# A four-block cross-attention transformer step: the first FFN's first two pairs of tiles moved into the last attention slot and its tail

## The chip, the cores and the metric

The kernel runs on one core of a Trainium2 chip. A core has four compute engines, each with its own instruction queue: TensorE (PE, matrix products, writes to PSUM only), VectorE (DVE), ScalarE (ACT) and GpSimd (POOL); SyncE (SP) issues DMAs. They run side by side and wait for each other through semaphores. The metric is the device time of one execution in microseconds, the median of several runs.

## The reference

The input x is 4 batches of 512 tokens of 128 features. Four blocks follow, each with a cross-attention (16 heads of 8, 77 keys) and an FFN, each of a different kind:

```
x = x + tanh(g) * attention_l(layernorm(x), ctx)      # l = 0..3
x = x + tanh(g) * ffn_l(layernorm(x))
```

What matters here is the end of the first attention and the first FFN. Its three products have both operands rounded to a 4-bit grid in blocks of 16 values:

```
def fp4_quant_dequant(x):        # blocks of 16 along the last dim
    scale = max(|xb|) / 6;  q = nearest of {0,.5,1,1.5,2,3,4,6} * sign * scale
gate = q(x) @ q(w_gate).T;   y = q(x) @ q(w_up).T
h    = silu(gate) * y                                 # 352 wide
out  = q(h) @ q(w_down).T
```

So for each token the input is rounded, two products are made, silu and a product follow, the result is rounded again and multiplied down to 128 features.

## The kernel before

The 2048 tokens are 16 tiles of 128; a batch b has four tiles (TPB = 4). The attention of block l runs in slots k = -1 to 4, and each slot has NCH = 12 steps c. In slot k TensorE makes the turned scores of batch k (turned_scores), ScalarE their exponentials (weigh, L783), TensorE the weighted sums (L1665, in three groups, the last one in step 0 of the next slot), and, one slot later, the tail of batch k: turn_sums (transposes of the sums), VectorE's normalise, att_transposed, ScalarE's attT_out, project, and VectorE's residual_read and residual with the statistics of the next layer norm. Slot k = B = 4 holds only the tail of batch 3. GpSimd refines the inverse deviation (refine, L582 to L585) and makes the shift (shift), and ScalarE normalises with them (normalise_out, L724).

The FFN of block 0 (ffn0 on each engine) goes by pairs of tiles, j = 0 to 7. For a pair:

- TensorE: up(2j), up(2j+1) (L1747, L1748: gate and up products into banks 0 to 3). An fp32 product shows as two records of the trace.
- ScalarE: silu of both tiles (L850).
- VectorE: product(j) (L1326), its blockwise maximum (L1330), rounded(j): the 4-bit rounding in eight operations (L981 to L983, L973 to L977).
- GpSimd: one multiplication with the scales (L677).
- TensorE and ScalarE: turn(i) (L1755, transposes in bank 4), hT_out(i) (L854, L855), down(i) (L1764), for the tiles of a pair two turns of the loop later. There is one bank for the turned tiles, so turn(i) waits for hT_out(i - 1).

product(j) for j >= 2 waits for the turns up to tile 2j - 3, and up(2j) waits for product(j - 1). Behind rounded(3) and rounded(5) stand residual(0) and residual(1) on VectorE; in turns j = 5 and 7 TensorE also makes the input and the queries of block 1 (turn_input, queries).

The FFN's input, batch by batch, has its own rounding. Batches 0 to 2 are jobs 3 to 5, shared between VectorE (job_scales, L994 and L981 to L983; job_steps, L1001 and L1002) and GpSimd (quantise_begun, quantise_ended, L609 to L616), in slots 2, 3 and 4. Batch 3 is done by VectorE alone in ten operations, quantise_batch(3) (L1098 to L1101), behind product(1). Then input_transposed(b) (TensorE, L1737) and xqT_out(b) (ScalarE, L844) turn a batch; they stand in turns j = 0, 1, 3 and 5 of the FFN's loop.

Every engine carries out its instructions in the order in which the program issues them, and that order is written by hand: functions such as after(k, c) on VectorE say what comes in which step. An instruction that waits holds all that is behind it on its engine.

Of the kernel before, what the change touches and what calls it, by code (L numbers as in the profile page):

```python
# [94 lines left out]
def program(nc, a, out):  # L95
    with ExitStack() as ctx:
# [223 lines left out]
        def tail_bank(n, h): return 7 if n == N - 1 and h == 1 else 3  # L320
# [178 lines left out]
        def _(pool):  # L499
# [117 lines left out]

            pool.wait_ge(ld_const, 16)
# [12 lines left out]
            for l in range(L):  # L631
                for k in range(-2, B + 1):
                    n = l * B + k
                    if l == 0 and k == 1:
                        quantise_begun(2)
                        quantise_ended(2)
                    if 0 <= k < B and n + 2 < N and n + 2 >= 3 * B:
                        mask_rows(n + 2)
                    if 0 <= k < B and n + 3 < N:
                        key_rows(n + 3)  # L640
                    if 0 <= k + 1 < B:
                        split_maxima(n + 1)
                    if l == 0 and k == 0:
                        for j in range(2):
                            quantise_begun(j)
                            quantise_ended(j)
                    if l == 0 and k >= 2:
                        quantise_begun(k + 1)
                        quantise_ended(k + 1)
                    if l == 2 and k == -1:  # L650
                        refine((5, B - 1))
                        shift((5, B - 1))
                    if l == 2 and k == -1:
                        pool.wait_ge(am_w_part, 1)
                        pool.partition_all_reduce(am[:, 3:4], am[:, 1:2], P, RMAX).then_inc(am_w_all, 1)
                    if l == 0 and k in (-1, 1, 3):
                        mask_parts((k + 1) // 2)
                    if l == 1 and k in (-1, 0, 2):
                        mask_parts((3, 4, 0, 5)[k + 1])
                    if l == 1 and k == 1:  # L660
                        last_masks()
                    if l == 2 and k == 0:
                        split_experts(gH, gL, 0)
                    if l == 2 and k == 1:
                        split_experts(uH, uL, 1)
                    if k >= 1:
                        refine((2 * l + (l > 1) + 1, k - 1))
                        if l == 0:
                            shift((1, k - 1))
                    if l == 3 and 1 <= k <= 3:  # L670
                        split_down(k - 1)
                if l == 0:
                    for j in range(T // 2):
                        h = fh[:, j % 2, :, :].rearrange("p t (n e) -> p (t n) e", e=16)
                        v = qh[:, j % 2, 0, :].rearrange("p (n e) -> p n e", e=16)
                        pool.wait_ge(hq_scaled, j + 1)
                        pool.tensor_tensor(h, v, hscale[:, j % 2, :].unsqueeze(2).to_broadcast([P, 44, 16]),  # L677
                                           ALU.mult).then_inc(hq_done, 1)
# [18 lines left out]
        def _(act):  # L697
# [54 lines left out]
            def attention(l):  # L752
# [50 lines left out]
                for k in range(-1, last + 1):  # L803
                    for c in range(NCH):
# [35 lines left out]

            def ffn0(xT_one, q_one):
                def xqT_out(b):
                    act.wait_ge(xqT_ps, b + 1)
                    act.activation(xnT[:, b, :], ps[:, 5, :], ACT.Copy).then_inc(xqT_ready, 1)  # L844

                def silu(i):
                    act.wait_ge(gu_ps, i + 1)
                    if i >= 2:
                        act.wait_ge(h_done, i // 2)
                    act.activation(fsg[:, i % 2, :], ps[:, i % 2, 0:FI], ACT.Silu).then_inc(silu_done, 1)  # L850

# [4 lines left out]
                for j in range(T // 2 + 2):  # L856
                    if j == 0 or j % 2 == 1 and j < 6:
                        xqT_out((j + 1) // 2)
# [5 lines left out]
                    if j == 0:  # L864
                        normalise_out((1, B - 1))
# [102 lines left out]
        def _(dve):  # L968
# [231 lines left out]

            def attention(l):
# [18 lines left out]
                def residual_read(b):  # L1220
# [3 lines left out]
                    y = ps[:, 3, :].rearrange("p (t d) -> p t d", d=D)  # L1224
# [16 lines left out]
                def after(k, c):  # L1241
# [77 lines left out]
            def ffn0(q_rest, maximum):  # L1319
                def product(j):  # L1320

                    h = fh[:, j % 2, :, :]
                    dve.wait_ge(silu_done, 2 * j + 2)
                    if j >= 2:
                        dve.wait_ge(hqT_ps, 2 * j - 2)
                    dve.tensor_tensor(h, ps[:, 2:4, 0:FI], fsg[:, :, :], ALU.mult).then_inc(h_done, 1)  # L1326
                    dve.wait_ge(h_done, j + 1)
                    if j >= 2:
                        dve.wait_ge(hq_done, j - 1)
                    link(dve.tensor_reduce(hscale[:, j % 2, :], h.rearrange("p t (n e) -> p (t n) e", e=16), AX_X, ALU.max,  # L1330
                                           apply_absolute_value=True))

                def rounded(j):

                    v = fh[:, j % 2, :, :].rearrange("p t (n e) -> p (t n) e", e=16)
                    w = [qh[:, j % 2, i, :].rearrange("p (b e) -> p b e", e=16) for i in range(2)]
                    link(quant_scales(hscale[:, j % 2, :], qs[:, 1, :]))
                    quant_steps(w, v, qs[:, 1, :].unsqueeze(2).to_broadcast([P, 44, 16])).then_inc(hq_scaled, 1)
                    dve.wait_ge(hq_scaled, j + 1)

                def residual(b):
                    xs = x[:, b * TPB:(b + 1) * TPB, :]
                    dve.wait_ge(f0_ps, b + 1)
                    dve.scalar_tensor_tensor(out=xs, in0=ps[:, 6 + b % 2, :].rearrange("p (t d) -> p t d", d=D),
                                             scalar=tg[:, 4:5], in1=xs, op0=ALU.mult, op1=ALU.add).then_inc(f0_done, 1)
                    dve.wait_ge(f0_done, b + 1)
                    next_input(1, b)
                    refine_own((2, b))
# [152 lines left out]
        def _(pe):  # L1501
# [68 lines left out]
            def attention(l):  # L1570
# [114 lines left out]
                for k in range(-1, B + (l < 3)):  # L1685
# [6 lines left out]
                    for c in range(NCH):  # L1692
# [35 lines left out]

            def ffn0(turn_input, queries, scores):
                pe.wait_ge(wqT_ready, 1)  # L1730

                def input_transposed(b):
                    pe.wait_ge(xq_done, b + 1)
                    if b >= 1:
                        pe.wait_ge(xqT_ready, b)
                    for i in range(TPB):
                        ins = pe.transpose(ps[:, 5, i * P:(i + 1) * P], xn[:, b * TPB + i, :], ident[:, :])  # L1737
                    ins.then_inc(xqT_ps, 1)

                def up(i):  # L1740
                    b, q = i // TPB, slice(i % TPB * P, (i % TPB + 1) * P)
                    pe.wait_ge(xqT_ready, b + 1)
                    if i == 1:
                        pe.wait_ge(y_done, B)
                    if i >= 2:
                        pe.wait_ge(h_done, i // 2)
                    pe.matmul(ps[:, i % 2, 0:FI], xnT[:, b, q], wqt[:, 0, :], start=True, stop=True)  # L1747
                    pe.matmul(ps[:, 2 + i % 2, 0:FI], xnT[:, b, q], wqt[:, 1, :], start=True, stop=True).then_inc(gu_ps, 1)  # L1748
# [22 lines left out]
                for j in range(T // 2 + 2):  # L1771
                    if j == 0 or j % 2 == 1 and j < 6:
# [236 lines left out]
```

## Time and profile before

| | |
|---|---|
| median of 3 runs | 832.74 us (832.41 to 835.34) |
| the profiled execution | 834.32 us |
| its span in the trace | 832.5 us |
| TensorE busy | 638.8 us (77%) |
| VectorE busy | 543.0 us (65%) |
| ScalarE busy | 326.1 us (39%) |
| GpSimd busy | 261.4 us (31%) |
| mean DMA rate | 81 GB/s |

Busy shares are averages over the whole span. The stretch that the change touches, from the last attention slot of block 0 to the end of its FFN, lies between about 103 and 225 us. The rows of a timeline give the start and the length of a group of instructions in microseconds, the engine, the line of the kernel, the operation with the tiles it writes and reads, and in square brackets the idle time of the engine before it and what ended that. The granted clock of TensorE is given as a share of its full 2.4 GHz.

### The profile page before, as it was taken

The numbers are of one execution on the slowest core, as the hardware profiler recorded it, in microseconds if no ns is written. First come the engines' busy times: TensorE is split into PE (matmuls) and PEld (weight loads), VectorE is DVE, ScalarE is ACT, GpSimd is POOL, SyncE is SP. The second block draws the span as 40 slices with busy tenths as digits, with TensorE's granted clock in tenths as the row PEclk, the third lists the DMA queues.
The fourth block names the chain that finished last, engine by engine and source line by source line (L and its number), as shares of the span: only waits on it lengthen the run. The fifth ranks groups of instructions, "written<-read, shape, count | busy, mean of one in ns | idle before, by whom it ended". The sixth has DMA issues, their size and how long they took to land. (4 is left out here: it accounts for less than half of the span.)

```text
span 832.5 us, 9949 instructions
## 1 busy us (share of the span) xinstructions
PE 638.8 (77%) x2926; PEld 397.5 (48%) x2926; DVE 543.0 (65%) x1451; ACT 326.1 (39%) x627; POOL 261.4 (31%) x470
## 2 busy tenths in 40 slices
PE   5788775566779998884888870348887898989997
PEld 3433333354665564552534330124343576767875
DVE  8775635888772553485736655863558798878655
ACT  3044552233224344353143440214544455545554
POOL 4343365111011312113250721001122445445463
PEclk9577987688869999896599985555998899999999
DMA  8864311002204323006044320222500232333341
GB/s 253 187 177 132 73 37 46 2 0 64 63 12 140 90 41 91 1 1 182 9 123 156 57 76 0 62 64 67 169 6 2 63 103 93 103 113 106 112 121 57
DMA packets 67989, 67.71 MB, mean 81 GB/s; under 512 B 25119, under 2 KB 48223, under 8 KB 67552
## 3 DMA queue, kind: packets, MB, share of 16 engines
q1 hardware_dynamic: 61326, 64.61, 28.4%
q10 hardware_dynamic: 6610, 2.47, 1.2%
q8 instruction: 24, 0.39, 0.2%
q14 instruction: 29, 0.24, 0.1%
HBM read 50.29 MB, written 17.60 MB: 82 GB/s over the span
## 5 line engine op out<-in xcount | busy, mean ns | idle before, releaser
L783 ACT ACTIVATE PT<-ps 110x512 f32<-110x512 f32 x192 | 110.5, 595 | 137.3 <-PE ps L1645 63.4
L1217 DVE TENSOR_REDUCE mraw<-ps 128x4 f32<-128x308 f32 x256 | 116.0, 476 | 73.6 <-PE ps L1605 23.7
L1605 PE MATMUL ps<-KG,QG 98*128 98x308 f32 x256 | 113.0, 477 | 49.4 <-DVE mraw L1217 34.1
L693 POOL TENSOR_TENSOR sg<-sg,cb 128x512 f32<-128x512 f32 x64 | 83.8, 1312 | 78.3 <-ACT sg L945 74.9
L1605 PEld LDWEIGHTS ps<-KG,QG 98*128 98x128 f32 x256 | 59.2, 237 | 94.4 <-DVE mraw L1217 70.4
L1645 PE MATMUL ps<-QG,KG 128*110 128x512 f32 x192 | 93.1, 506 | 9.1 <-ACT PT L783 6.7
L1461 DVE TENSOR_TENSOR ps<-ps,sg 128x512 f32<-128x512 f32 x72 | 50.3, 698 | 39.3 <-POOL sg L693 36.3
L1665 PE MATMUL ps<-PT,VN 128*18 128x512 f32 x512 | 73.0, 644 | 0.0
L525 POOL CAST mhl<-mraw 128x64 fp32r<-128x64 f32 x16 | 5.0, 310 | 192.7 <-DVE mraw L1217 180.0
L945 ACT ACTIVATE sg<-ps 128x512 f32<-128x512 f32 x72 | 43.0, 597 | 46.4 <-PE ps L1864 45.7
L1645 PEld LDWEIGHTS ps<-QG,KG 128*110 128x110 f32 x192 | 35.0, 187 | 54.4 <-ACT PT L783 38.8
L932 ACT ACTIVATE hH<-ps 128x512 fp32r<-128x512 f32 x72 | 43.0, 597 | 37.7 <-DVE ps L1461 36.2
L582 POOL TENSOR_TENSOR nt<-nhv,rs 128x4 f32<-128x4 f32 (+1 forms) x63 | 14.8, 236 | 129.9 <-DVE rs L1057 126.6
L1107 DVE RECIPROCAL rden<-ps 128x32 f32<-128x32 f32 x32 | 11.3, 354 | 64.3 <-PE ps L1555 64.2
L1453 DVE TENSOR_TENSOR hL<-ps,hH 128x512 fp32r<-128x512 f32 x72 | 49.0, 681 | 0.7 <-ACT hH L932 0.6
L724 ACT ACTIVATE xn<-x,nsh,rs 128x128 f32<-128x128 f32 x64 | 26.3, 482 | 44.2 <-DVE nsh L1072 22.4
L1747 PE MATMUL ps<-wqt,xnT 128*128 128x352 f32 x32 | 19.0, 690 | 28.8 <-DVE fh L1326 28.1
L1882 PE MATMUL ps<-hH,dwH 128*128 128x512 f32 x72 | 29.7, 413 | 1.2 <-ACT hH L932 1.2
L677 POOL TENSOR_TENSOR fh<-qh,hscale 128x704 f32<-128x704 f32 x8 | 11.1, 1385 | 59.6 <-DVE qh L977 59.6
L1884 PE MATMUL ps<-hL,dwH 128*128 128x512 f32 x72 | 29.3, 406 | 0.0
L1883 PE MATMUL ps<-hH,dwL 128*128 128x512 f32 x72 | 29.2, 405 | 0.0
L1079 DVE TENSOR_SCALAR xn<-x,mv,rs 128x128 f32<-128x128 f32 x64 | 22.3, 412 | 9.5 <-POOL rs L585 9.4
(284 smaller groups left out, 1414.9 us busy)
## 6 DMA issues: line engine op xcount, KB each, us to landing
cb<-c_parts SPq DMA_DIRECT2D x64, 256.0 KB, 3.3
QG<-q_parts SPq DMA_DIRECT2D x48, 256.0 KB, 3.9
KG<-k_parts SPq DMA_DIRECT2D x48, 154.0 KB, 3.0
q_parts<-hiT SPq DMA_DIRECT2D x14, 256.0 KB, 2.0
q_parts<-loT SPq DMA_DIRECT2D x14, 256.0 KB, 2.3
k_parts<-kmH SPq DMA_DIRECT2D x16, 154.0 KB, 2.4
k_parts<-kmL SPq DMA_DIRECT2D x16, 154.0 KB, 2.6
VN<-v_parts SPq DMA_DIRECT2D x16, 144.0 KB, 2.9
```

Of the source, the lines that this page charges most:

```text
L693: pool.tensor_tensor(sg[:, n % 3, :], sg[:, n % 3, :], cb[:, k % CRING, :], ALU.mult).then_inc(sc_done, 1)
L783: act.activation(PT[0:w, q % PTR, :], ps[0:w, 4 + q % 2, :], ACT.Exp, scale=SCALE[l]).then_inc(exp_done, 1)
L932: act.activation(hH[:, n % 3, :], ps[:, up_bank(n), :], ACT.Copy).then_inc(h_hi, 1)
L945: act.activation(sg[:, n % 3, :], ps[:, n % 2, :], ACT.Silu).then_inc(s3_done, 1)
L1217: dve.tensor_reduce(mraw[:, n % 2, i, g * HG:(g + 1) * HG], ps[:, u % 2, 0:GK].rearrange("p (h k) -> p h k", k=K), AX_X, ALU.max).then_inc ...
L1453: dve.tensor_tensor(hL[:, n % 3, :], ps[:, up_bank(n), :], hH[:, n % 3, :].bitcast(F32), ALU.subtract).then_inc(h_lo, 1)
L1461: dve.tensor_tensor(ps[:, up_bank(n), :], ps[:, up_bank(n), :], sg[:, n % 3, :], ALU.mult).then_inc(a1_done, 1)
L1605: ins = pe.matmul(o, QG[0:KS, n % 3, g, q], KG[0:KS, n % 3, g, :], start=True, stop=l not in (1, 2))
L1645: ins = pe.matmul(o, KG[:, n % 3, g, r], QG[:, n % 3, g, :], start=True, stop=l not in (1, 2))
L1665: pe.matmul(ps[p0:p0 + VC, 6 + f, :], VN[:, n % 3, g * 4 + PAIRS.index((t, j)), :], PT[:, q % PTR, :], start=s == 0, stop=s == 1, skip_gro ...
L1882: pe.matmul(o, dwH[:, e, :], hH[:, r, :], start=e == NE, stop=False)
L1884: pe.matmul(o, dwH[:, e, :], hL[:, r, :], start=False, stop=e == NE - 1).then_inc(f3_step, 1)
```

## The change

On TensorE, input_transposed(0) comes behind project(2) in slot 3, up(0) and up(1) in steps 8 and 10 of slot 3, up(2) and up(3) in steps 5 and 7 of slot 4. On ScalarE, xqT_out(0) is in step 7 of slot 3, the first two silus in step 2 and the next two in step 6 of slot 4; normalise_out((1, 2)) moves from step 3 to step 6 of slot 4, normalise_out((1, 3)) from the end of turn 0 to behind the silus of turn 3. On VectorE, product(0) and rounded(0) come in step 3 of slot 4, ahead of residual_read(3). On GpSimd the multiplication of the first pair comes ahead of refine((1, 3)). Batch 2 is no longer a shared job: quantise_batch(2) takes the place of quantise_batch(3), which moves behind product(4). The sums of batch 3 are turned in bank 4 instead of 3, and batch 0 in bank 2 instead of 5. The functions that both places call are moved out of ffn0 unchanged and left out here.

```diff
-        def tail_bank(n, h): return 7 if n == N - 1 and h == 1 else 3
+        def tail_bank(n, h): return 4 if n == B - 1 else 7 if n == N - 1 and h == 1 else 3
+        def xq_bank(b): return 2 if b == 0 else 5
...
@@ gpsimd @@
-                    if l == 0 and k >= 2:
+                    if l == 0 and k in (2, 3):
                         quantise_begun(k + 1)
                         quantise_ended(k + 1)
+                    if l == 0 and k == B:
+                        multiply(0)
...
-                    for j in range(T // 2):
+                    for j in range(1, T // 2):
+                        multiply(j)
...
@@ scalar @@
-                        if c == 3 and k >= 2 and l == 0:
+                        if c == (6 if k == B else 3) and k >= 2 and l == 0:
                             normalise_out((1, k - 2))
+                        if c == 7 and k == B - 1 and l == 0:
+                            xqT_out(0)
+                        if k == B and l == 0 and c in (2, 6):
+                            silu(c // 3)
+                            silu(c // 3 + 1)
...
-                for j in range(T // 2 + 2):
-                    if j == 0 or j % 2 == 1 and j < 6:
+                xqT_out(1)
+                for j in range(2, T // 2 + 2):
+                    if j in (3, 5):
                         xqT_out((j + 1) // 2)
...
-                    if j == 0:
+                    if j == 3:
                         normalise_out((1, B - 1))
...
@@ vector @@
             def quantise_batch(b):
...
-                wait_job(dve, 5)
+                wait_job(dve, 4)
...
-                    if c in (4, 7) and l == 0 and k - 2 >= 0:
+                    if c in (4, 7) and l == 0 and k in (2, 3):
                         (job_scales if c == 4 else job_steps)(k + 1)
+                    if c == 3 and l == 0 and k == B:
+                        product(0)
+                        rounded(0)
...
-                for j in range(T // 2):
+                for j in range(1, T // 2):
                     product(j)
                     if j == 1:
-                        quantise_batch(B - 1)
+                        quantise_batch(2)
+                    if j == 4:
+                        quantise_batch(3)
                     rounded(j)
...
@@ tensor @@
             def turn_sums(n, h):
                 pe.wait_ge(o_out, 2 * n + h + 1)
+                if n == B - 1 and h == 0:
+                    pe.wait_ge(exp_done, NCH * n + NCH - 1)
...
+                        if c == 5 and k == B and l == 0:
+                            up(2)
                         if c == 6 and k >= 1:
                             project(l * B + k - 1)
+                        if c == 7 and k == B and l == 0:
+                            up(3)
+                        if c == 6 and k == B - 1 and l == 0:
+                            input_transposed(0)
+                        if c in (8, 10) and k == B - 1 and l == 0:
+                            up(c // 2 - 4)
...
                 def turn(i):
                     pe.wait_ge(hq_done, i // 2 + 1)
+                    if i == 0:
+                        pe.wait_ge(y_done, B)
...
-                for j in range(T // 2 + 2):
-                    if j == 0 or j % 2 == 1 and j < 6:
+                input_transposed(1)
+                for j in range(2, T // 2 + 2):
+                    if j in (3, 5):
                         input_transposed((j + 1) // 2)
```

## Rows read from the trace of the kernel before

**Rows 1.** The timeline of VectorE, 122 to 149 us: start, length, engine, line, idle before

```profile
128.87 0.69 DVE L994 TENSOR_REDUCE qs<-xn 128x32 f32<-128x512 f32 x1 [6.17 <-ACT xn L724]
...
131.41 0.69 DVE L1227 TENSOR_TENSOR yb<-ps,rows 128x512 f32<-128x512 f32 x1 [1.03 <-PE ps L1567]
...
134.59 0.42 DVE L1001 TENSOR_SCALAR qw<-qw 128x512 int32<-128x512 int32 x1
...
137.93 0.89 DVE L1326 TENSOR_TENSOR fh<-ps,fsg 128x704 f32<-128x704 f32 x1 [2.46 <-ACT fsg L850]
...
143.66 0.89 DVE L977 TENSOR_TENSOR qh<-qh 128x704 f32<-128x704 f32 x1
148.75 0.89 DVE L1326 TENSOR_TENSOR fh<-ps,fsg 128x704 f32<-128x704 f32 x1 [4.20 <-ACT fsg L850]
```

**Rows 2.** The timeline of VectorE, inside the first FFN

```profile
150.59 0.69 DVE L1098 TENSOR_REDUCE qs<-xn 128x32 f32<-128x512 f32 x1
...
155.96 0.19 DVE L981 TENSOR_SCALAR hscale<-hscale 128x44 f32<-128x44 f32 x1
...
160.77 0.89 DVE L1326 TENSOR_TENSOR fh<-ps,fsg 128x704 f32<-128x704 f32 x1
...
168.85 0.89 DVE L1326 TENSOR_TENSOR fh<-ps,fsg 128x704 f32<-128x704 f32 x1 [1.47 <-PE ps L1755]
...
180.15 0.89 DVE L1326 TENSOR_TENSOR fh<-ps,fsg 128x704 f32<-128x704 f32 x1
...
188.18 0.89 DVE L1326 TENSOR_TENSOR fh<-ps,fsg 128x704 f32<-128x704 f32 x1 [1.41 <-PE ps L1755]
```

**Rows 3.** The timeline of TensorE, second half of the last attention slot

```profile
111.96 1.34 PE L1567 MATMUL ps<-wp,attT 128*128 128x128 f32 x8 [0.48 <-ACT attT L735]
...
116.96 0.96 PE L1645 MATMUL ps<-QG,KG 128*110 128x512 f32 x2 [0.43 <-ACT PT L783]
...
119.38 1.05 PE L1665 MATMUL ps<-PT,VN 128*18 128x512 f32 x8
```

**Rows 4.** Busy time in stretches of 2 us: engines, then TensorE's granted clock, DMA

```profile
114.00:116.00 2.00, 2.00 (x9) 0.40 (x2) 1.90 (x10) 0.36 (x1) 0.00 (x0) 0.50 0.00 0
...
118.00:120.00 2.00, 2.00 (x20) 0.53 (x12) 0.48 (x2) 0.85 (x2) 1.92 (x2) 1.00 0.00 0
```

**Rows 5.** The timeline of ScalarE: end of the attention, and the switch at 646 us

```profile
120.58 0.60 ACT L731 ACTIVATE o_sb<-ps 114x512 f32<-114x512 f32 x1 [1.73 <-PE ps L1665]
...
646.00 1.28 ACT L945 ACT_TABLE_LOAD   x1
647.29 0.60 ACT L945 ACTIVATE sg<-ps 128x512 f32<-128x512 f32 x1
```

**Rows 6.** The timeline of TensorE around the FFN: transposes, up projections, turns

```profile
131.16 1.06 PE L1737 MATMUL ps<-ident,xn 128*128 128x128 f32 x4
...
161.81 1.51 PE L1747 MATMUL ps<-wqt,xnT 128*128 128x352 f32 x2 [4.74 <-DVE fh L1326]
...
166.63 0.84 PE L1755 MATMUL ps<-ident,fh 128*128 128x128 f32 x3
...
168.20 0.52 PE L1755 MATMUL ps<-ident,fh 128*128 128x128 f32 x3
...
169.89 0.83 PE L1747 MATMUL ps<-wqt,xnT 128*128 128x352 f32 x2 [0.50 <-DVE fh L1326]
...
172.33 0.49 PE L1755 MATMUL ps<-ident,fh 128*128 128x128 f32 x3
...
181.18 1.51 PE L1747 MATMUL ps<-wqt,xnT 128*128 128x352 f32 x2 [5.98 <-DVE fh L1326]
...
185.25 0.60 PE L1579 MATMUL ps<-ident,xn 128*128 128x128 f32 x4
```

**Rows 7.** The timeline of ScalarE: one normalisation, and the copy before the fourth product

```profile
127.11 1.65 ACT L724 ACTIVATE xn<-x,nsh,rs 128x128 f32<-128x128 f32 x4 [5.94 <-POOL nsh L596]
...
167.79 0.26 ACT L855 ACTIVATE hqT<-ps 96x128 f32<-96x128 f32 x1
```

More of the change, by code:

```diff
@@ L839, in ffn_weights_out, with xqT_out, silu @@
                 act.activation(wdT[0:96, 2, :], ps[0:96, 2, 256:384], ACT.Identity).then_inc(wqT_ready, 1)
-            def ffn0(xT_one, q_one):
[L842 to L850, printed above, removed]
+            def xqT_out(b):
+                act.wait_ge(xqT_ps, b + 1)
+                act.activation(xnT[:, b, :], ps[:, xq_bank(b), :], ACT.Copy).then_inc(xqT_ready, 1)
+            def silu(i):
+                act.wait_ge(gu_ps, i + 1)
+                if i >= 2:
+                    act.wait_ge(h_done, i // 2)
+                act.activation(fsg[:, i % 2, :], ps[:, i % 2, 0:FI], ACT.Silu).then_inc(silu_done, 1)
+            def ffn0(xT_one, q_one):
                 def hT_out(i):
@@ L1199, in scores_out, with product, rounded, residual @@
                 link(dve.reciprocal(sco[:, ts, :], sco[:, ts, :]))
+            def product(j):
+                h = fh[:, j % 2, :, :]
+                dve.wait_ge(silu_done, 2 * j + 2)
+                if j >= 2:
+                    dve.wait_ge(hqT_ps, 2 * j - 2)
+                dve.tensor_tensor(h, ps[:, 2:4, 0:FI], fsg[:, :, :], ALU.mult).then_inc(h_done, 1)
+                dve.wait_ge(h_done, j + 1)
+                if j >= 2:
+                    dve.wait_ge(hq_done, j - 1)
+                link(dve.tensor_reduce(hscale[:, j % 2, :], h.rearrange("p t (n e) -> p (t n) e", e=16), AX_X, ALU.max,
+                                       apply_absolute_value=True))
+            def rounded(j):
+                v = fh[:, j % 2, :, :].rearrange("p t (n e) -> p (t n) e", e=16)
+                w = [qh[:, j % 2, i, :].rearrange("p (b e) -> p b e", e=16) for i in range(2)]
+                link(quant_scales(hscale[:, j % 2, :], qs[:, 1, :]))
+                quant_steps(w, v, qs[:, 1, :].unsqueeze(2).to_broadcast([P, 44, 16])).then_inc(hq_scaled, 1)
+                dve.wait_ge(hq_scaled, j + 1)
+            def residual(b):
+                xs = x[:, b * TPB:(b + 1) * TPB, :]
+                dve.wait_ge(f0_ps, b + 1)
+                dve.scalar_tensor_tensor(out=xs, in0=ps[:, 6 + b % 2, :].rearrange("p (t d) -> p t d", d=D),
+                                         scalar=tg[:, 4:5], in1=xs, op0=ALU.mult, op1=ALU.add).then_inc(f0_done, 1)
+                dve.wait_ge(f0_done, b + 1)
+                next_input(1, b)
+                refine_own((2, b))
             def attention(l):
@@ L1223, in residual_read @@
                     xs = x[:, b * TPB:(b + 1) * TPB, :]
-                    y = ps[:, 3, :].rearrange("p (t d) -> p t d", d=D)
+                    y = ps[:, tail_bank(n, 1), :].rearrange("p (t d) -> p t d", d=D)
                     dve.wait_ge(y_ps, n + 1)
@@ L1727, in attention, with input_transposed, up @@
                         weighted_sums(3, 1, 1)
-            def ffn0(turn_input, queries, scores):
[L1730 to L1748, printed above, removed]
+            def input_transposed(b):
+                pe.wait_ge(xq_done, b + 1)
+                if b == 0:
+                    pe.wait_ge(wqT_ready, 1)
+                else:
+                    pe.wait_ge(xqT_ready, b)
+                for i in range(TPB):
+                    ins = pe.transpose(ps[:, xq_bank(b), i * P:(i + 1) * P], xn[:, b * TPB + i, :], ident[:, :])
+                ins.then_inc(xqT_ps, 1)
+            def up(i):
+                b, q = i // TPB, slice(i % TPB * P, (i % TPB + 1) * P)
+                pe.wait_ge(xqT_ready, b + 1)
+                if i == 1:
+                    pe.wait_ge(y_done, B - 1)
+                if i >= 2:
+                    pe.wait_ge(h_done, i // 2)
+                pe.matmul(ps[:, i % 2, 0:FI], xnT[:, b, q], wqt[:, 0, :], start=True, stop=True)
+                pe.matmul(ps[:, 2 + i % 2, 0:FI], xnT[:, b, q], wqt[:, 1, :], start=True, stop=True).then_inc(gu_ps, 1)
+            def ffn0(turn_input, queries, scores):
                 def turn(i):
                     pe.wait_ge(hq_done, i // 2 + 1)
+                    if i == 0:
+                        pe.wait_ge(y_done, B)
                     if i >= 1:
```

36 lines of the change are left out of this document (6 added, 30 removed).

## The prediction

> **What bounds the kernel now.** The page comes first: TensorE is busy for 77% of the span and VectorE for 65%, but these are averages over stages with different limits, so the question is which engine ends last in the stretch that the diff touches. The timeline of VectorE answers it. From the second product of the FFN at 148.75 us on, one VectorE operation follows the next, through quantise_batch, rounded and the next product [rows 2]; its only pauses there are those before the 4th, 6th and 8th product, 1.47 and 1.41 us in the first two, and both wait for a transpose of TensorE (L1755). So the FFN is bound by VectorE, with three short hand-overs to TensorE. Ahead of 148.75 it is different: VectorE stands idle for 6.17 us (waiting for ScalarE's normalised tiles, which wait for GpSimd's shift), 1.03 us, 2.46 us and 4.20 us [rows 1]. The change puts work into these gaps. TensorE (windows) has holes there too, and its granted clock goes from 0.50, which is 1.2 GHz, at 114 to 116 us to 1.00, 2.4 GHz, at 118 to 120 us [rows 4]. Nothing of DMA is in the chain here. All that follows the FFN waits for its last VectorE work, so I take a microsecond won at its end to be one won at the end of the program.
>
> I count product(j), the VectorE multiplication of L1326, as a mile post. Before they stand at 137.93, 148.75, 160.77, 168.85, 180.15 and 188.18 us for j = 0 to 5 [rows 1, 2].
>
> **Part 1, what goes into the last attention slot.** TensorE gets, behind project(2), four transposes (input_transposed(0)), then up(0) and up(1) between the score matmuls. Four transposes took 1.06 us at 1.2 GHz [rows 6]. Two up steps took 166.63 - 161.81 = 4.82 us at 1.2 GHz and 172.33 - 169.89 = 2.44 us at 2.4 GHz [rows 6]. The transposes fall at about 113 us, where the clock is low, the up steps behind 116 us, where it is high [rows 4]: 1.06 + 2.44 = 3.50 us of new work in TensorE's queue. Of this 0.43 us goes into the wait at 116.96 [rows 3], and about 0.45 us is given back as the work behind 116 us now runs at the higher clock for longer and the next exponentials are ready when TensorE comes to them (my estimate from the same rows). The last weighted sum, which ended at 119.38 + 1.05 = 120.43 us [rows 3], ends at 123.0. Cost: 2.6 us at the head of the tail, with bounds of 1.5 us (more of the work in waits) and 5.0 us (up steps at 1.2 GHz). Behind TensorE's inserted work are queued the scores, and ScalarE's exponentials wait for these; ScalarE's xqT_out(0) is 0.6 us between two exponentials, in time in which it waits for TensorE.
>
> The bank moves (tail_bank 3 to 4 for the last batch, xq_bank 2) add one wait: turn_sums(3, 0) needs the 11th exponential of the slot. That is done before TensorE gets through up(1), the last scores and four sums, so it costs nothing; without that cover it would cost one exponential, 0.6 us. SP and its DMAs are not moved.
>
> **Part 2, product(0) and rounded(0) in the gap.** ScalarE's sums_out(3, 1) began at 120.58, 0.15 behind the sums, and took 0.60 [rows 5]; now it ends at 123.8. Then comes the table switch for Silu. The only other place where a Silu was ready at once is 646.00: the load took 1.28 us, and the Silu began at 647.29 [rows 5]. Two Silus of 0.46 us, overlapping, give 0.80: product(0) starts at 125.95. product(0), the reduction and rounded(0) took 143.66 + 0.89 - 137.93 = 6.62 us [rows 1], so VectorE is free at 132.6. Behind it wait residual_read(3) and residual(3), whose y lands at about 131 us, since project(3) now stands behind up(2) in TensorE's queue (2.4 us at worst, as VectorE is busy until 132.6 that costs nothing). They took 134.59 - 131.41 = 3.2 us [rows 1]. job_scales(5) and job_steps(5), some 2.3 us of VectorE, are gone. product(1) starts at 135.8, if up(2), up(3) and their Silus are done. Between them on ScalarE stands normalise_out((1, 2)), ready at 127.11 as before and 1.65 us long [rows 7]; at the low clock up(3) ends at about 133.3 and its Silu at 133.8, 2 us early. Gain at product(1): 148.75 - 135.8 = 12.95 us. On GpSimd multiply(0) now stands before refine((1, 3)): its result is needed only by normalise_out((1, 3)), some 15 us later. It costs nothing.
>
> (The Trainium skill, page "ScalarE: Activation LUTs", section "What ACT_TABLE_LOAD costs", gives a switch about 1.38 us of drain beside the 1.28 us of load, 2.66 in all. In this trace no pause is seen between load and Silu at 646. By the page's sum product(0) and all behind it would start 1.4 us later, and the time would be 829.8.)
>
> **Part 3, product(1) to product(3).** quantise_batch(2) takes the place of quantise_batch(3), the same operations, 155.96 - 150.59 = 5.37 us [rows 2]; product(2) starts 12.02 us after product(1), at 147.8. From product(2) to product(3) it was 8.08 us, with the 1.47 us wait for turn(3). ScalarE now has normalise_out((1, 3)) between silu(7) and the copies of the first turn. The copy ended at 167.79 + 0.26 = 168.05 and turn(3) began at 168.20 [rows 6, 7]: no slack. Most of the 1.65 us comes through: 1.4 us. The sum uses 1.4, with bounds 0.6 (the up steps ahead of it at a better clock) and 1.65. product(3) starts at 157.3, and 11.3 us later product(4), at 168.6.
>
> **Part 4, quantise_batch(3) behind product(4).** This is 5.37 us of VectorE that was hidden in part before, as job 5, and no longer is. It also brings a new wait: input_transposed(3) is the first in TensorE's queue in turn j = 5, and it needs xq_done 4. Behind it are queued up(10), up(11), turn_input(0), turn(6), down(5), queries(0) and turn(7), and product(5) waits for turn(7). From the start of product(4): 148.75 to 150.59, 1.84 us for product and reduction [rows 1, 2], 5.37 for the quantisation, 0.14 to TensorE, 1.0 for the transposes at 1.2 GHz, the two up steps, and 188.18 - 185.25 = 2.93 us for what follows [rows 2, 6]. TensorE has been idle for some 8 us by then; after 5.98 us of idleness the two steps took 185.25 - 181.18 = 4.07, after 4.74 us they took 4.82 [rows 6]. With the transposes ahead of them, which use up some of the slow time, I take 4.0: 15.3 us, bounds 13.3 (all at 2.4 GHz) and 16.1. VectorE alone would need 1.84 + 5.37 + 4.81 = 12.0. It was 188.18 - 180.15 = 8.03 us, so this costs 7.3 us, of which 3.3 are the new wait. product(5) starts at 183.9.
>
> **The sum.** 12.95 - 1.4 - 7.3 = 4.3 us gained at product(5). From there to the end of the FFN the two kernels do the same in the same order. The profiled execution took 834.32 us (span 832.5 and 1.8 around it), which gives 830.0; the median of the runs is 832.74, 1.6 below the profiled one, and I apply the same gain to it: **828.4 us**. Bounds on the gain from the terms: 5.0 instead of 2.6 in part 1 leaves 1.9, with 16.1 in part 4 1.1; 1.5, 0.6 and 13.3 at the kind ends give 8.2.
>
> **Rivals.**
> (a) Kind clock: TensorE is at 2.4 GHz when quantise_batch(3) ends, and the fourth product doesn't feel the normalisation. Then 12.95 - 5.3 = 7.65 gained: 825.1. For it: the pauses before are filled. Against it: TensorE has nothing to do for the 8 us ahead of input_transposed(3), and after idle times of 4.74 and 5.98 us it came back slow.
> (b) Low clock in the tail, ending on the other side. If the inserted work keeps the clock at 1.2 GHz from 116 us to 123 us, the up steps cost 2.4 us more and the 4.2 us of attention matmuls in that stretch another 4.2: 6.6 us, so the change is 2.3 us slower, 835.0. It decides from 4.3 us on, about two thirds of that stretch at the low clock. Against it: TensorE gets denser here, not emptier, and the clock rose at about 116 us under just such a load [rows 4]. A third of it is likelier and lies within the range.
> (c) The gap is not there: if product(0) came as late as residual(3) anyway (a late Silu, say), only the change of where the batches are quantised is left: 5.37 on VectorE for some 2.3, and the new waits, 3.1 + 3.3 + 1.4 us: over 840. The gap of 6.17 us stands plainly in the trace, so this has little chance.
> (d) The Silu behind the table load starts late. At 646 us it did not [rows 5]; a pause as long as the load itself, 1.28 us, would give 829.7. By the page of the Trainium skill named in part 2 this is what happens.
>
> **How the numbers follow.** The forecast with its own scatter (gain 2.5 to 6.5 us) 0.65; partly low clock (gain 0 to 2.5) 0.12; (a) 0.11; (d) 0.06; (b) 0.04; (c) 0.02. Half a per cent is 4.2 us, about what a measurement of this kernel can tell from no change, and the forecast stands almost on it. Over 4.2 us gained: a bit over half of the forecast, and (a): 0.46. Slower by over 0.5%: (c) and the far end of (b): 0.04. Same: 0.50. The range leaves out the far ends of (a), (b) and (c): 825.0 to 832.0.
>
> **What would show it.** In the changed profile product(0) should start near 126 us, product(1) 135.8, product(2) 147.8, product(3) 157.3, product(4) 168.6, product(5) 183.9. The wait before the second FFN product should be gone, that before the fourth about 2.9 us (1.47 before), and before the sixth about 3.3 us (1.41 before), with input_transposed(3) waiting for VectorE. The last weighted sum should end near 123. I would be wrong if the clock's row for 116 to 122 us stayed at 0.50, if a pause stood between the table load and the first Silu, or if a wait behind product(5) grew.

## The result and the profile after

The changed kernel took 828.45 us (median of 17 runs), the kernel before 834.18 us in runs beside it. The ratio is 0.9935, with a 95% interval of 0.9913 to 0.9957: 5.4 us faster (3.6 to 7.3). Here and below, runs over 1.5% longer than the fastest of their kernel are left out of the ratio. The profiled execution has a span of 828.7 us.

VectorE's timeline of the changed kernel, the first FFN's products and what stands beside them (start, length, line, idle before), answers to [rows 1, 2]:

```profile
124.96 0.89 DVE L1221 TENSOR_TENSOR fh<-ps,fsg 128x704 f32<-128x704 f32 x1 [0.65 <-ACT fsg L862]
...
132.36 1.26 DVE L1280 SCALAR_TENSOR_TENSOR x<-yb,tg,x 128x512 f32<-128x512 f32 x1
...
135.33 0.88 DVE L1221 TENSOR_TENSOR fh<-ps,fsg 128x704 f32<-128x704 f32 x1
...
147.36 0.89 DVE L1221 TENSOR_TENSOR fh<-ps,fsg 128x704 f32<-128x704 f32 x1
...
156.69 0.89 DVE L1221 TENSOR_TENSOR fh<-ps,fsg 128x704 f32<-128x704 f32 x1 [2.71 <-PE ps L1787]
...
167.98 0.89 DVE L1221 TENSOR_TENSOR fh<-ps,fsg 128x704 f32<-128x704 f32 x1
...
183.89 0.89 DVE L1221 TENSOR_TENSOR fh<-ps,fsg 128x704 f32<-128x704 f32 x1 [3.93 <-PE ps L1787]
...
204.58 0.89 DVE L1221 TENSOR_TENSOR fh<-ps,fsg 128x704 f32<-128x704 f32 x1 [2.12 <-PE ps L1787]
```

The gaps of 6.17, 2.46 and 4.20 us of [rows 1] are gone up to 0.65 us before product(0), and product(0) starts 13 us sooner (14.2 us counted from project(2), as below). Three waits are left, as before, but longer: 2.71, 3.93 and 2.12 us where there were 1.47, 1.41 and 1.67.

TensorE and ScalarE of the changed kernel, for [rows 3, 5, 6, 7]: project(2), the first up step in the slot, the last sums, the turn of batch 3, then the table load with the Silus and the normalisation of turn 3 with the copy behind it.

```profile
113.21 1.16 PE L1589 MATMUL ps<-wp,attT 128*128 128x128 f32 x8 [0.49 <-ACT attT L743]
...
116.27 0.80 PE L1776 MATMUL ps<-wqt,xnT 128*128 128x352 f32 x2
...
121.00 1.05 PE L1687 MATMUL ps<-PT,VN 128*18 128x512 f32 x8
...
175.22 1.12 PE L1766 MATMUL ps<-ident,xn 128*128 128x128 f32 x4 [12.61 <-DVE xn L1115]
...
122.20 0.60 ACT L739 ACTIVATE o_sb<-ps 114x512 f32<-114x512 f32 x1 [2.02 <-PE ps L1687]
...
122.81 1.28 ACT L862 ACT_TABLE_LOAD   x1
...
124.11 0.82 ACT L862 ACTIVATE fsg<-ps 128x352 f32<-128x352 f32 x2
...
153.83 1.64 ACT L732 ACTIVATE xn<-x,nsh,rs 128x128 f32<-128x128 f32 x4
...
155.37 0.37 ACT L867 ACTIVATE hqT<-ps 128x256 f32<-128x256 f32 x1
```

And the granted clock of the slot, for [rows 4]: 1.00 throughout, where it was 0.50 for a part before.

```profile
112.00:122.00 10.00, 9.27 (x54) 4.57 (x54) 5.86 (x21) 5.48 (x11) 4.35 (x4) 1.00 0.00 0
```

The row at 175.22 is input_transposed(3): TensorE had stood idle for 12.61 us before it, waiting for quantise_batch(3).

Upstream of the change the profiles differ by themselves. project(2) of slot 3 started at 111.96 us before, at 113.21 after, and at up to 119.43 in the experiments, though nothing was changed ahead of it. So all profiles are compared by distances inside the stretch, from the start of project(2):

| us | before | after | after, again |
|---|---|---|---|
| project(2) to end of last sums | 8.47 | 8.84 | 8.82 |
| project(2) to product(0) | 25.97 | 11.75 | 11.73 |
| product(0) to product(1) | 10.82 | 10.37 | 10.35 |
| product(2) to product(3) | 8.08 | 9.33 | 8.60 |
| product(4) to product(5) | 8.03 | 15.91 | 15.45 |
| project(2) to first exponential of block 1 | 135.74 | 130.21 | 129.04 |

The last row is read from these two lines of ScalarE, before and after:

```profile
247.70 0.60 ACT L783 ACTIVATE PT<-ps 110x512 f32<-110x512 f32 x1 [0.49 <-PE ps L1649]
...
243.42 0.60 ACT L791 ACTIVATE PT<-ps 110x512 f32<-110x512 f32 x1 [0.49 <-PE ps L1671]
```

By it the change wins 5.5 and 6.7 us by the start of block 1's weighing, and the times say 5.4 and, in the second set of runs, 6.5 (ratio 0.9923, 0.9890 to 0.9956). What is won in the stretch arrives at the end. The kernel before has one profile only, so how its own distances vary is not known.

### The profile page after: what moved, and what is told of

It reads as the page before. It is cut to its first block and busy times, and to the rows that moved or that the text cites. A ratio compares the mean times of both kernels' runs of the same rounds, so it can differ in the third digit from the quotient of the medians.

```text
span 828.7 us, 9949 instructions
## 1 busy us (share of the span) xinstructions
PE 637.4 (77%) x2926; PEld 397.2 (48%) x2926; DVE 546.5 (66%) x1455; ACT 326.6 (39%) x627; POOL 255.5 (31%) x466
```

## The experiments

All are edits of the changed kernel; ratios are to the kernel before, timed beside them. The theory is that of the prediction: VectorE bounds the FFN, the tail's gap takes in the first pair, and two new waits take a part of it back, one behind a normalisation on ScalarE and one behind the late rounding of batch 3. The rivals are that the gap alone is the gain, that TensorE's inserted steps cost the attention, and that the waits are TensorE's low clock.

**The control.** No edit.

> The changed kernel itself once more, on the chip of these runs: 0.9935 as in its first runs, with product(0) to product(7) at the same distances as in its first profile except where the granted clock differs. It says how far the steps of part 1, 3 and 4 move with the phase of the clock: product(2) to product(3) 8.3 to 9.4 us, product(4) to product(5) 14.5 to 16 us.

Ratio 0.9923 (0.9890 to 0.9956). The distances are in the table: the same within 0.02 us where TensorE is not waited for, and 0.73 and 0.46 us apart in the two steps named, which end with a wait for it; both lie in the expected ranges. That is the least scatter to allow for: where later profiles have the order of the changed kernel from product(4) to product(5), they take down to 14.5 us for it (part 4 below).

**The filled gap.** product(0) and rounded(0) go behind residual(3):

```diff
-                    if c == 3 and l == 0 and k == B:
+                    if c == 7 and l == 0 and k == B:
                         product(0)
                         rounded(0)
...
-                        if c == 5 and k == B and l == 0:
-                            up(2)
...
                         if c == 7 and k == B and l == 0:
+                            up(2)
                             up(3)
```

> The changed kernel with product(0) and rounded(0) behind residual(3) again, and up(2) behind project(3); up(0), up(1) and their Silus stay in the attention's last slot and tail. It says what filling VectorE's gap of 6 us is worth by itself. Theory: project(3) is no longer behind up(2) and the normalisation is gone from its path, so y lands at 127.6 on the changed kernel's scale, residual(3) is done at 130.8, product(0) starts there and product(1) at 137.5 against 135.33: 2.1 us of the gain are lost, ratio 0.996. Rival (the filled gap is the gain): all of 6.6 us, product(0) with its rounding, come back, and the kernel is slower than before, ratio 1.001.

```profile
128.77 1.05 PE L1687 MATMUL ps<-PT,VN 128*18 128x512 f32 x8
...
136.17 0.75 DVE L1280 SCALAR_TENSOR_TENSOR x<-yb,tg,x 128x512 f32<-128x512 f32 x1
...
138.62 0.88 DVE L1221 TENSOR_TENSOR fh<-ps,fsg 128x704 f32<-128x704 f32 x1
...
145.27 0.89 DVE L1221 TENSOR_TENSOR fh<-ps,fsg 128x704 f32<-128x704 f32 x1
```

The last sums ended at 129.82 us in this profile; product(1) comes 15.45 us behind them, against 135.33 - 122.05 = 13.28 in the changed kernel (and 148.75 - 120.43 = 28.32 before). So putting the first pair ahead of the residual is worth 2.2 us, as the theory had it (2.1). The other 12.9 us at product(1) come from what both versions share: TensorE's and ScalarE's first pairs done early, and no shared rounding of batch 2 between the tail and the FFN. No run takes these apart. The ratio, 0.9976 (0.9938 to 1.0014), holds both the theory's 0.996 and the rival's 1.001; the trace decides. (The span of this profile, 842.8 us, is not used. Inside the stretch it shows nothing unusual: product(1) to product(2) is 12.05 us and product(3) to product(4) 11.29, as in the changed kernel.)

**The normalisation ahead of the copies.** normalise_out((1, 3)) moves behind them:

```diff
-                    if j == 3:
-                        normalise_out((1, B - 1))
...
                         hT_out(2 * j - 3)
+                    if j == 3:
+                        normalise_out((1, B - 1))
```

> The changed kernel with normalise_out((1, 3)) behind both copies of turn 3 instead of ahead of them. Theory (the fourth product waits for turn(3), which waits for a copy that stands behind the 1.65 us normalisation): VectorE's wait before product(3) falls from 2.71 us to about 1.4, and the span by 1.3 us. Rival (turn(3) is late for TensorE's low clock alone): the wait stays at 2.7 us and nothing moves. In the times, a ratio to the kernel before of 0.992 against 0.9935.

```profile
151.23 0.89 DVE L1221 TENSOR_TENSOR fh<-ps,fsg 128x704 f32<-128x704 f32 x1
...
158.27 0.89 DVE L1221 TENSOR_TENSOR fh<-ps,fsg 128x704 f32<-128x704 f32 x1 [0.42 <-PE ps L1787]
...
152.27 0.83 PE L1776 MATMUL ps<-wqt,xnT 128*128 128x352 f32 x2 [4.02 <-DVE fh L1221]
...
154.99 1.38 PE L1777 MATMUL ps<-wqt,xnT 128*128 128x352 f32 x2
...
156.16 0.73 PE L1787 MATMUL ps<-ident,fh 128*128 128x128 f32 x3
```

The wait is 0.42 us instead of 2.71, more than the 1.3 expected. The TensorE rows say why: up(6) starts at the high clock here (0.83 us for the first pair of records, against 1.51 in [rows 6]) and falls to the low one within the steps. From the start of up(6) to the first turned tile it was 3.89 us, to 156.16, against 4.83 in the changed kernel (148.40 to 153.23), 0.94 us less. What is left, 2.29 - 0.94 = 1.35 us, is the normalisation. Against the control it comes out alike: its wait was 1.98 us and its first turned tile 0.24 us later behind product(2), which leaves 1.32. The ratio, 0.9943 (0.9912 to 0.9975), can't tell 1.3 us.

**The turn of batch 3 and its wait.** In turn 5 it goes behind the turned tiles, and with it the input and queries of block 1:

```diff
-                    if j in (3, 5):
-                        input_transposed((j + 1) // 2)
+                    if j == 3:
+                        input_transposed(2)
...
                         turn(2 * j - 3)
                         down(2 * j - 4)
+                    if j == 5:
+                        input_transposed(3)
+                        turn_input(0)
+                        queries(0)
```

with ScalarE's copies in the same order.

> The changed kernel with the turn of batch 3 (input_transposed(3) with its wait for xq_done 4) and the input and queries of batch 0 of the next block behind turn(7) and down(6) in turn j = 5, on TensorE and ScalarE alike. Theory (the 3.93 us before product(5) come from the queue behind that wait): the wait before product(5) is gone, product(4) to product(5) falls from 15.91 to 12.0 us, and 3.9 us are won, a ratio to the kernel before of 0.989. Rival (they are spent in the next block instead, since the queries of its batch 0 come later and their DMAs are on the path): product(5) is earlier all the same, but the first weighted sums of block 1 are not, and the ratio stays at 0.9935.

```profile
173.59 0.89 DVE L1226 TENSOR_TENSOR fh<-ps,fsg 128x704 f32<-128x704 f32 x1
...
185.61 0.89 DVE L1226 TENSOR_TENSOR fh<-ps,fsg 128x704 f32<-128x704 f32 x1
...
174.62 1.51 PE L1781 MATMUL ps<-wqt,xnT 128*128 128x352 f32 x2 [6.42 <-DVE fh L1226]
...
177.10 1.38 PE L1781 MATMUL ps<-wqt,xnT 128*128 128x352 f32 x2
```

The wait is gone, and product(4) to product(5) is 12.02 us, exactly VectorE's own work. The up steps ran at the low clock here too (1.51 and 1.38 us), so without the queue behind input_transposed(3) the low clock makes no wait here; it only sets how long that queue takes. The ratio is 0.9890 (0.9844 to 0.9936), as expected, though its interval overlaps the changed kernel's. project(2) to the first exponential of block 1 is 128.03 us with the low clock in the slot (below), which by itself costs 1.5; with that taken off it is 3.7 and 2.5 us less than in the two profiles of the changed kernel, whose waits were 3.93 and 3.47. So most of it arrives, and the rival, that the later queries give it back, falls; both7 below confirms it.

**The rounding itself.** quantise_batch(3) is replaced by a copy; the 4-bit rounding of batch 3's input is left out.

```diff
+                if b == 3:
+                    xb = xn[:, b * TPB:(b + 1) * TPB, :]
+                    dve.tensor_scalar(xb, xb, 1.0, None, ALU.mult).then_inc(xq_done, 1)
+                    dve.wait_ge(xq_done, b + 1)
+                    return
```

> The changed kernel with the ten operations of quantise_batch(3) replaced by one copy of the tiles onto themselves (0.43 us); the 4-bit rounding of batch 3's input is left out, which changes the output for that batch. It measures all that stands behind product(4) for that rounding. Theory (5.37 us of VectorE plus the new wait): product(4) to product(5) falls from 15.91 to about 9.5 us, since input_transposed(3) is ready at 2.3 us behind product(4) and the chain of TensorE from there takes 7.2: 6.4 us faster than the changed kernel, ratio 0.986. Rival (only VectorE's own work counts, the wait was there anyhow): 4.9 us, ratio 0.988.

```profile
173.49 0.89 DVE L1226 TENSOR_TENSOR fh<-ps,fsg 128x704 f32<-128x704 f32 x1
...
183.51 0.89 DVE L1226 TENSOR_TENSOR fh<-ps,fsg 128x704 f32<-128x704 f32 x1 [2.94 <-PE ps L1792]
```

product(4) to product(5) is 10.02 us, 5.9 less than the changed kernel's 15.91 and 5.4 less than the control's 15.45; expected were 6.4 by the theory and 4.9 by the rival, so this run lies between and does not separate them, and a wait of 2.94 us is left in it. turn5 separates them: moving the transposition alone takes away the whole wait of 3.9 us without taking any work from VectorE. The ratio is 0.9894 (0.9853 to 0.9935).

**TensorE's steps in the attention's slot.** up(0) and up(1) go to steps 1 and 3 of slot 4:

```diff
-                        if c in (8, 10) and k == B - 1 and l == 0:
-                            up(c // 2 - 4)
+                        if c in (1, 3) and k == B and l == 0:
+                            up(c // 2)
```

> The changed kernel with up(0) and up(1) not among the scores of slot 3 but in steps 1 and 3 of slot 4, behind the last weighted sums. It measures what TensorE's inserted work costs the attention. From project(2) of slot 3 to the end of the last sums the changed kernel took 8.84 us in its profile and 10.4 us in three of the profiles since, where the clock was low in part of it. Theory (2.4 us of up steps push the sums, as part 1 of the prediction has it): project(2) to the last sums shortens by 2.0 to 2.4 us, and product(0) comes 1.0 to 1.6 us sooner after project(2), as the up steps now take part of the time of the table load: ratio 0.992. Rival (the steps fill waits of TensorE between the scores and cost the sums under 1 us): the sums end at most 1 us sooner, product(0) comes later by the 2.4 us of the steps less the table load, and the ratio is 0.994 or above.

```profile
112.27 1.16 PE L1589 MATMUL ps<-wp,attT 128*128 128x128 f32 x8 [0.48 <-ACT attT L743]
...
120.17 1.05 PE L1687 MATMUL ps<-PT,VN 128*18 128x512 f32 x8
...
124.72 0.89 DVE L1221 TENSOR_TENSOR fh<-ps,fsg 128x704 f32<-128x704 f32 x1 [0.88 <-ACT fsg L862]
```

The clock was low in this slot from 113 to 117 us. project(2) to the last sums is 121.22 - 112.27 = 8.95 us, product(0) 12.45. Profiles of the changed order with the clock low just behind project(2) (there are seven) have 10.36 to 10.40 and, the run with the gap left open aside, 13.3 up to product(0). Here is the granted clock of one of them, the normalisation's run, in the third number from the end (0.50 is 1.2 GHz; project(2) began at 115.56):

```profile
116.00:118.00 2.00, 2.00 (x12) 2.00 (x11) 0.40 (x1) 0.00 (x0) 0.81 (x1) 0.50 0.00 0
...
118.00:120.00 2.00, 2.00 (x12) 0.54 (x11) 1.91 (x6) 1.08 (x2) 0.00 (x0) 0.73 0.00 0
```

So at the same clock the two up steps cost the sums 1.4 us, and moving them wins 0.85 us at product(0). The theory had 2.0 to 2.4 and 1.0 to 1.6: the direction is right, the size smaller. The rival's under 1 us is missed as well. The ratio is 0.9900 (0.9865 to 0.9935), which can't be told from the changed kernel's.

**Both moves, and the same for turn 7.**

> Both of the moves before in one kernel (normalise_out((1, 3)) behind the copies of turn 3; the turn of batch 3 and the input and queries of the next block behind the turned tiles in turn 5), and the latter for turn 7 too. Theory: the waits before product(3), product(5) and product(7) fall from 2.7, 3.9 and 2.1 us to about 1.4, 0 and 1.2; 1.3 + 3.9 + 0.9 = 6.1 us faster than the changed kernel, a ratio to the kernel before of 0.986. Rival (later queries of the next block hold its first scores): the products are early, but the first exponential of block 1 isn't, and the ratio is 0.990 or above.

Its edit is that of the two runs together, with turn_input(1) and queries(1) of turn 7 behind the turned tiles as well.

```profile
161.87 0.89 DVE L1225 TENSOR_TENSOR fh<-ps,fsg 128x704 f32<-128x704 f32 x1 [0.42 <-PE ps L1791]
...
185.18 0.89 DVE L1225 TENSOR_TENSOR fh<-ps,fsg 128x704 f32<-128x704 f32 x1
...
204.01 0.89 DVE L1225 TENSOR_TENSOR fh<-ps,fsg 128x704 f32<-128x704 f32 x1 [0.28 <-PE ps L1791]
```

The waits before product(3), (5) and (7) are 0.42, 0 and 0.28 us, project(2) to the first exponential of block 1 122.99 us: 7.2 and 6.1 less than in the two profiles of the changed kernel, 12.8 less than before. So the rival falls. Ratio 0.9879 (0.9831 to 0.9927); 0.986 was expected and lies inside.

**The clock behind the last two waits.** Products that nobody reads fill TensorE's idle time before up(6) and up(14):

```diff
+                    if j in (3, 7):
+                        pe.wait_ge(hqT_ready, 2 * j - 4)
+                        for i in range(10 if j == 3 else 15):
+                            pe.matmul(ps[:, 4, :], ident[:, :], xnT[:, 0, :], start=True, stop=True)
```

> The kernel of both moves with products that nobody reads (10 of 128x512 in turn 3, 15 in turn 7, into the bank of the turned tiles) in the 5 and 7 us in which TensorE has nothing to do. Theory (what is left of the waits before product(3) and product(7) is TensorE at 1.2 GHz after its idle time): the granted clock is 1.00 when up(6) and up(14) start, the two steps take 2.4 instead of 4.8 us, and both waits, 2.6 us in all, are gone: 0.983. Rival (the clock falls all the same, or the products that nobody reads last longer than the gap and hold up(6)): the waits stay or grow, 0.986 to 0.990.

```profile
147.62 8.75 PE L1815 MATMUL ps<-xnT,ident 128*128 128x512 f32 x20
...
156.21 0.76 PE L1780 MATMUL ps<-wqt,xnT 128*128 128x352 f32 x2
...
160.47 0.89 DVE L1225 TENSOR_TENSOR fh<-ps,fsg 128x704 f32<-128x704 f32 x1 [2.09 <-PE ps L1791]
...
209.03 0.89 DVE L1225 TENSOR_TENSOR fh<-ps,fsg 128x704 f32<-128x704 f32 x1 [6.72 <-PE ps L1791]
```

The rival's second half: 10 of them took 8.75 us, and up(6), which could have started at about 152.8 (product(2) ended at 152.65), started at 156.21. The waits grew to 2.09 and 6.72 us, and the ratio is 0.9928 (0.9905 to 0.9952). But up(6) ran at the high clock. So the size was the mistake, not the cause, and the next run has 4 and 6 of them.

> The kernel of both moves with 4 and 6 products that nobody reads instead of 10 and 15. In the last profile one of them took 0.87 us, so 10 took 8.75 us in a gap of 5.0 us and held up(6) till 156.2; now they take 3.5 and 5.2 us in gaps of 5.0 and 6.3 us. Theory (TensorE's low clock after its idle time is what is left of the waits): with the clock at 1.00 up(6), up(7) take 2.4 us, product(2) to product(3) and product(6) to product(7) are 6.6 us, the length of VectorE's own work, and both waits are 0; about 1 us faster than the kernel of both moves by its profile (its waits were 0.42 and 0.28), up to 2.6 us where its clock is low from the start of the steps: ratio 0.986. Rival (a gap of 1.2 us is enough for the clock to fall, or the products delay others): waits of 1.4 us, ratio 0.988.

```profile
149.82 3.60 PE L1815 MATMUL ps<-xnT,ident 128*128 128x512 f32 x8
...
155.15 0.83 PE L1780 MATMUL ps<-wqt,xnT 128*128 128x352 f32 x2 [1.73 <-DVE fh L1225]
...
156.41 0.76 PE L1780 MATMUL ps<-wqt,xnT 128*128 128x352 f32 x2
...
154.11 0.89 DVE L1225 TENSOR_TENSOR fh<-ps,fsg 128x704 f32<-128x704 f32 x1
...
160.76 0.89 DVE L1225 TENSOR_TENSOR fh<-ps,fsg 128x704 f32<-128x704 f32 x1
...
196.03 0.89 DVE L1225 TENSOR_TENSOR fh<-ps,fsg 128x704 f32<-128x704 f32 x1
...
202.68 0.89 DVE L1225 TENSOR_TENSOR fh<-ps,fsg 128x704 f32<-128x704 f32 x1
```

The two steps take 0.83 and 0.76 us per pair of records, and both distances, product(2) to (3) and (6) to (7), are 6.65 us, with no wait at all. The granted clock stays at 1.00 through both gaps, here and in the next run, where without these products it fell within the up steps or before them (both7: 0.71 and 0.50 in the 4 us from 156 us on). So the last waits were TensorE at 1.2 GHz after its idle time. Ratio 0.9851 (0.9805 to 0.9897).

**Everything together**, with up(0) and up(1) in slot 4:

> The last kernel with up(0) and up(1) in steps 1 and 3 of slot 4 as well: the fastest version that the runs point to. At the low clock in the slot product(0) came 12.45 us behind project(2) with the steps there, and 13.3 us without. Theory: the gains add, 0.85 us more, product(0) at 12.4 and product(7) 71 us behind it, ratio 0.985. Rival (they do not, as the tail then waits for the up steps): product(0) at 13.3 us or later, ratio 0.987 or above.

```profile
114.29 2.06 PE L1593 MATMUL ps<-wp,attT 128*128 128x128 f32 x8 [0.48 <-ACT attT L743]
...
126.75 0.89 DVE L1225 TENSOR_TENSOR fh<-ps,fsg 128x704 f32<-128x704 f32 x1 [0.88 <-ACT fsg L862]
...
197.68 0.89 DVE L1225 TENSOR_TENSOR fh<-ps,fsg 128x704 f32<-128x704 f32 x1
```

project(2), at 114.29 us, to product(0) is 12.46 us (12.4 expected), product(0) to product(7) 70.93, and project(2) to the first exponential of block 1 121.33 us, 14.4 less than before and 0.55 less than in warm_sized (121.88). The median is 824.35 us, with 837.88 for the kernel before beside it, the ratio 0.9833 (0.9792 to 0.9874), which is 14.0 us of 837.88: again what the distances say. This is the fastest version measured; against the changed kernel its interval is clear. warm_sized and all_three can't be told apart by the times.

## Why the prediction was right, point by point

**Part 1, the cost of TensorE's steps in the slot** was 2.6 us in the sum and is mis-sized. The changed kernel's sums end 8.84 us behind project(2), 0.4 more than before. Two things are mixed in this: in the kernel before the clock was low for 3.5 us of the slot and in the changed kernel's profile it was not. With the clock low in both it is 10.39 against 8.47, 1.9 us, of which the up steps are 1.4 (ups_tail) where the sum put in 2.4; so at the same clock the term was 0.7 too large, and against the 0.4 of this profile 2.2. The range for it, 1.5 to 5.0, misses the high-clock case: that the clock could be better than in the one profile of before was not in the bounds. Why the clock stayed up in two profiles of this order and fell in seven is not shown.

**Part 2** held: the sums' end to product(0) was 2.95 us in the sum and 124.96 - 122.05 = 2.91 in the trace. There is no pause behind the table load: it starts at 122.81 and takes 1.28, the Silu starts at 124.11. (The drain of about 1.38 us that the Trainium skill names, page "ScalarE: Activation LUTs", section "What ACT_TABLE_LOAD costs", does not show; rival (d) falls.) product(0) to product(1) was 9.85 in the sum and 10.37 in the trace. Half a microsecond is missing in one instruction, residual(3)'s update of x: 1.26 us at 132.36, against 0.75 us as before. It runs while GpSimd does multiply(0), 1.39 us from 131.69, which the change puts there. In gap_open, where multiply(0) comes later, it took 0.75 us; in the nine other profiles, in which it stands beside multiply(0), 1.25 or 1.26. product(2) at 147.36, one of whose inputs lies in PSUM, kept its 0.89 us beside multiply(1):

```profile
131.69 1.39 POOL L625 TENSOR_TENSOR fh<-qh,hscale 128x704 f32<-128x704 f32 x1 [2.97 <-DVE qh L991]
...
147.41 1.39 POOL L625 TENSOR_TENSOR fh<-qh,hscale 128x704 f32<-128x704 f32 x1 [7.45 <-DVE qh L991]
```

"It costs nothing" was wrong for this step: what a GpSimd instruction does to VectorE beside it had not been asked. (The Trainium skill, page "GPSIMD Engine Reference", section "1. Specifications", names just this: its SBUF interface is shared with VectorE where an instruction has two SBUF inputs. The trace agrees.)

**Part 3**: the wait before product(3) was to be about 2.9 us and was 2.71 and 1.98. norm_later puts 1.35 us of it on the normalisation (1.4 in the sum); the rest is the low clock, as warm_sized shows, where it is gone.

**Part 4**: product(4) to product(5) was 15.3 us in the sum and 15.91 and 15.45 in the traces, with a wait of 3.93 and 3.47 (3.3 in the sum). The mechanism is as told: turn5 takes it away whole. The two up steps took 180.82 - 176.12 = 4.70 us where the sum had 4.0, and 4.39 in the control. In the three other profiles with this order they took 3.78, 3.46 and 3.54 us (norm_later, gap_open, ups_tail), as the clock rose within them, and product(4) to product(5) was 14.84, 14.53 and 14.60 us. So 4.0 was about the middle of five draws, and the 0.6 us by which this profile missed 15.3 are the clock. One reading was wrong: TensorE's idle time before input_transposed(3) was put at some 8 us and was 12.61, since TensorE ran out of work 5.4 us before product(4).

**The sum.** Predicted were 4.3 us of gain, measured are 5.4 (3.6 to 7.3) and 6.5 (3.7 to 9.2). The errors at product(5), counted from project(2): +2.2 us for part 1 (1.5 of it the clock, 0.7 the size), -0.5 for the collision on VectorE, +0.15 in part 3, -0.6 in part 4: 4.3 + 1.25 = 5.5 us, which is what the two profiles show, (188.18 - 111.96) - (183.89 - 113.21) = 5.54. The forecast was closer than its terms, as errors of both signs met in it. product(5) stood at 183.89 us, at 183.9 in the prediction; that is a coincidence, since project(2) started 1.25 us late in that profile. So is the median of 828.45 beside 828.4, as the kernel before took 834.18 in those runs and not 832.74. By the chances a change of less than half a per cent was the likeliest (0.50, against 0.46 for faster); the measured ratio lies on the other side of that line, its interval on both.

Rival (a), no such waits, is what all_three made true by other edits. Rival (b) did not come: in the two profiles of the changed kernel the clock stayed up in the slot, and in seven others it fell only for a few microseconds behind project(2), as it did before. Rival (c) did not come either, and its price was wrong: gap_open puts product(0) behind residual(3), which is what (c) supposes, and that loses 2.2 us at product(1), where (c) had the kernel slower than before, at over 840 us.

## What to carry to other kernels

When a step moves ahead in one engine's queue, look at the instruction that now stands first behind a wait, and at everything queued behind it that somebody else needs: here half of what the late rounding cost (3.9 of the 7.9 us by which product(4) to product(5) grew) was a transposition with no hurry that held the seven steps queued behind it. Work that nobody waits for goes behind the work that somebody waits for, on every engine of the chain. And count a gap's worth by leaving it open: the gap that looked like the gain was 2.2 of the 15.0 us won between the last sums and product(1).

## What the runs showed of the hardware

- Filling TensorE's idle time with products that nobody reads kept its clock: 4 products (3.6 us) in a gap of 5 us, with 1.7 us of idleness left, and the next two up steps took 2.4 us instead of 3.9 to 4.8. With 6 products before up(14) it was the same, and all four such gaps, of two profiles, ended at the high clock. One fp32 product of 128x512 from SBUF took 0.87 us at the high clock; with 10 of them in that gap the wait grew from 0.42 to 2.09 us.
- The state of the clock in the slot moved the end of the sums by 1.5 us between profiles of the same instruction order (8.82 and 8.84 against 10.36 to 10.40). For a term of a few microseconds one profile's clock is one draw.
- A VectorE instruction with two SBUF inputs (128x512) took 1.26 us beside a GpSimd multiplication of 128x704 and 0.75 us alone; one with an input in PSUM took its 0.89 us beside it as alone.
- The first 112 us, which no edit touched, varied by 7.5 us between profiles. TensorE's waits for DMAs into the query tiles are longer in the late ones (one of 4.9 us in both7 and of 6.0 in gap_open, none above 2.4 in the kernel before in the same stretch); why is not settled here.
